# Expert mixture of a transformer block: all eight experts for every token, or only each token's two experts, with rows routed on the chip

## The reference

```python
x = x + layernorm(attention(layernorm(x)))     # 16 heads, causal, ALiBi, projection w_proj
x = x + layernorm(ffn(layernorm(x)))

def ffn(x):                                    # 2048 tokens
    scores = sigmoid(xt @ gate_w.T)            # 8 experts
    _, sel = top_k(scores + expert_bias, 2)    # the two experts of each token
    # rows of xt times their score, sorted by expert, in bfloat16:
    # out_e = (silu(rows @ w1[e].T) * (rows @ w3[e].T)) @ w2[e].T, hidden width 352
    shared = silu(xt @ sw1.T) * (xt @ sw3.T) @ sw2.T      # float32
    return shared + (the two routed results of each token)
```

## Time and profile before

| what | value |
|---|---|
| time, median of 3 runs | 1047.0 us (1046.97 to 1048.84) |
| profiled execution: span from first to last instruction | 1044.3 us |
| PE busy | 960.0 us, 92% of the span |
| DVE, ACT, POOL busy | 550.3, 391.6, 195.1 us |
| stage three | 571.7 to 1044.3 us |

### The profile page before, as it was taken

How to read it: one execution, slowest core, us unless ns; L and a number is a source line. 1 busy time by engine, 2 the same in 40 slices (tenths; PEclk the granted TensorE clock), 3 DMA queues, 4 the chain that set the end, 5 groups by cost and what they waited for, 6 DMA issues and landing times.

```text
span 1044.3 us, 15975 instructions
## 1 busy us (share of the span) xinstructions
PE 960.0 (92%) x5053; PEld 527.7 (51%) x5080; DVE 550.3 (53%) x1238; ACT 391.6 (38%) x690; POOL 195.1 (19%) x151
## 2 busy tenths in 40 slices
PE   4999996899999999999998799999999899999994
PEld 4787764344444444444433464446444554446442
DVE  6444466556565655556325343845456644745554
ACT  4121211365656555565627320432123421442221
POOL 4200034142232223232010030103110130103000
PEclk9999998899999999999999899999999999999997
DMA  9999483533635333345220500114001130102001
GB/s 275 277 276 293 160 240 119 109 85 81 138 75 118 81 82 82 83 97 155 66 96 12 183 21 0 41 41 141 20 7 74 40 121 0 56 24 81 1 1 40
DMA packets 71105, 101.55 MB, mean 97 GB/s; under 512 B 25616, under 2 KB 38544, under 8 KB 70032
## 3 DMA queue, kind: packets, MB, share of 16 engines
q1 hardware_dynamic: 59264, 92.02, 30.4%
q0 software_dynamic: 11792, 8.95, 5.5%
HBM read 75.81 MB, written 33.69 MB: 105 GB/s over the span
## 4 chain that ended last, share of the span: by engine, by line
PE 74%; DVE 4%; issue 4%; DMA 1%; ACT 1%; SPq 1%; DVEq 0%; ACTq 0%
PE ps L1254 24%; PE ps L1353 13%; PE ps L1267 9%; PE ps L1437 8%; PE ps L1333 8%; PE ps L1456 4%; PE ps L1468 2%; PE ps L1336 2%; PE ps L1368 2%; PE ps L1484 1%; DMA k_st<-qk_split 1%; DVE scb_c L1148 1%; PE ps L1462 1%; DVE ps L965 0%; DMA iota_c<-in_iota 0%
## 5 line engine op out<-in xcount | busy, mean ns | idle before, releaser
L965 DVE CUSTOM_DVE_ANT_0 ps<-ps,alibi 128x1024 f32<-128x1024 f32 (+7 forms) x256 | 190.9, 779 | 148.1 <-PE ps L1267 144.3
L814 ACT ACTIVATE probs<-ps,key_bias 128x512 f32<-128x512 f32 (+3 forms) x384 | 201.3, 577 | 161.7 <-PE ps L1336 109.7
L1254 PE MATMUL ps<-xs,w13r 128*128 128x512 bf16 (+1 forms) x744 | 171.3, 379 | 3.0 <-PE ps L1456 0.9
L898 ACT ACTIVATE silu<-ps 128x512 f32<-128x512 f32 (+1 forms) x108 | 64.0, 595 | 274.5 <-PE ps L1254 274.4
L1353 PE MATMUL ps<-probs,ones 128*32 128x512 f32 (+3 forms) x768 | 164.1, 502 | 0.0
L1353 PE MATMUL ps<-probs,v_st 128*32 128x512 f32 (+3 forms) x768 | 164.1, 502 | 0.0
L678 POOL TENSOR_SCALAR alibi<-rel_b,slp 128x1024 f32<-128x1024 f32 x32 | 91.1, 2848 | 322.6 <-DVE rowmax L965 224.2
L1267 PE MATMUL ps<-k_st,q_st 96*128 96x512 f32 (+3 forms) x384 | 112.8, 384 | 22.5 <-DVE rowmax L965 13.2
L1333 PE MATMUL ps<-q_st,k_st 98*128 98x512 f32 (+3 forms) x384 | 126.2, 394 | 7.5 <-ACT probs L814 3.6
L1212 DVE TENSOR_TENSOR gr<-silu,ps 128x512 bf16<-128x512 f32 (+1 forms) x96 | 65.5, 685 | 117.9 <-PE ps L1254 112.9
L1254 PEld LDWEIGHTS ps<-xs,w13r 128*128 128x128 bf16 (+1 forms) x768 | 80.8, 106 | 89.6 <-issue 6.1
(11 more groups left out here) (125 smaller groups left out, 1130.6 us busy)
## 6 DMA issues: line engine op xcount, KB each, us to landing
qk_split<-qk_out SPq DMA_DIRECT2D x32, 512.0 KB, 7.7
q_st<-qk_split SPq DMA_DIRECT2D x48, 256.0 KB, 4.6
k_st<-qk_split SPq DMA_DIRECT2D x48, 256.0 KB, 6.5
w13r<-in_w POOLq DMA_DIRECT2D x16, 352.0 KB, 34.2
x_a<-in_x SPq DMA_DIRECT2D x4, 1024.0 KB, 8.0
v_rows<-v_out SPq DMA_DIRECT2D x16, 256.0 KB, 3.7
v_st<-v_rows SPq DMA_DIRECT2D x16, 256.0 KB, 6.9
attended<-raw SPq DMA_DIRECT2D x16, 256.0 KB, 5.8
```

Source lines behind the costliest of these rows:

```text
L814: act.activation(probs[:, v % 3, e, 0:width], ps[:, score_bank(v, e), 0:width], ACT.Exp, bias=key_bias[par][:, 2 * pair + e, j - 4 * qc + ...
L898: act.activation(silu[0:r, t % 2, :], ps[0:r, bank, :], ACT.Silu).then_inc(c_silu, 1)
L965: dve.tensor_tensor_reduce(scores, scores, alibi[h % 2][:, S - width:S], 1.0, -3e38, ALU.add, ALU.max, rowmax[:, h, i:i + 1]).then_inc(b_m ...
L1254: last = pe.matmul(dst, lhsT, rhs, start=start and n == 0, stop=stop and n == len(terms) - 1)
```

## The change

Tokens are no longer sent through all eight experts. For every chunk DVE computes, beside the two experts and their scores, the rank of each token among the tokens of its expert (PE makes the running counts with a triangular matrix of ones, unit `rank`), and from it a row in a DRAM region of that expert (`pos`). DVE writes the token's activations, scaled by the score, in bfloat16 (`xs`: eight tiles of 128 rows a chunk), and POOL scatters each tile with an indirect DMA. After all four chunks DVE works out a table (`table`): for each of 23 tiles of 256 rows, its expert and its first row. The number of tiles is fixed, for any distribution of the tokens. Then the unit `experts` runs: SP reads a row number from the table, loads the tile transposed, PE reads the expert's number and multiplies by that expert's weights, addressed by a register; ACT and DVE each copy half of the result to bfloat16 and SP stores it. Ranks are turned into rows of the result (`result_rows`) during this time. Last, POOL gathers each token's two result rows with eight indirect DMAs a chunk, DVE adds them to the shared expert's result, normalises, and POOL adds the residual.

The shared result of chunks 0 to 2 is kept in DRAM meanwhile (`keep`); the shared expert of chunk 3 is computed after the experts. The loop over chunks is written out as one list, `PLAN`. Nine more DMAs on POOL near the start write zeros into the regions. Attention and the stage before it are otherwise untouched.

The core of the diff (added lines; what they replace are the units in the section on the kernel before):

```diff
-FIRST = [("tr", 0), ("tr", 1), ("gate",), ("logits",)]
...
+TS = 256
+TILES = (2 * B * S + E * (TS - 1)) // TS
+REGION = TS + B * S
...
+PLAN = [("tr", 0, 0), ("tr", 0, 1), ("proj", 1, 0), ("hilo", 0), ("gate", 0), ("proj", 1, 1),
+        ("logits", 0), ("norm", 1, 0), ("root", 1, 0), ("route", 0), ("hid", 0, 0), ("norm", 1, 1),
+        ("x1", 1), ("rank", 0), ("pos", 0), ("xs", 0), ("hid", 0, 1), ("norm", 1, 3), ("norm", 1, 4),
+        ("root", 1, 1), ("heads", 2), ("hid", 0, 2), ("norm", 1, 5), ("sdown", 0), ("keep", 0),
+        ("tr", 1, 0), ("tr", 1, 1), ("hilo", 1), ("gate", 1), ("logits", 1), ("route", 1),
+        ("proj", 2, 0), ("proj", 2, 1), ("norm", 2, 0), ("root", 2, 0), ("heads", 3), ("hid", 1, 0),
+        ("norm", 2, 1), ("x1", 2), ("rank", 1), ("pos", 1), ("xs", 1), ("hid", 1, 1), ("norm", 2, 3),
+        ("norm", 2, 4), ("root", 2, 1), ("norm", 2, 5), ("proj", 3, 0), ("proj", 3, 1),
+        ("norm", 3, 0), ("root", 3, 0), ("hid", 1, 2), ("norm", 3, 1), ("x1", 3), ("sdown", 1),
+        ("norm", 3, 3), ("norm", 3, 4), ("root", 3, 1), ("keep", 1), ("tr", 2, 0), ("tr", 2, 1),
+        ("hilo", 2), ("gate", 2), ("logits", 2), ("route", 2), ("hid", 2, 0), ("norm", 3, 5),
+        ("rank", 2), ("pos", 2), ("xs", 2), ("tr", 3, 0), ("tr", 3, 1), ("gate", 3), ("logits", 3),
+        ("route", 3), ("hid", 2, 1), ("rank", 3), ("count",), ("pos", 3), ("table",), ("xs", 3),
+        ("hid", 2, 2), ("sdown", 2), ("keep", 2), ("experts",), ("hilo", 3), ("hid", 3, 0),
+        ("hid", 3, 1), ("hid", 3, 2), ("sdown", 3)]
...
+            def tile_in(s):
+                row = sp.value_load(tab_r[0:1, s:s + 1], min_val=0, max_val=ROWS - TS)
+                if s >= 3:
+                    sp.wait_ge(e_first, MT * (s - 2))
+                sp.dma_start_transpose(xsT[:, s % 3, :, :], xs_d[bass.ds(row, TS), :]
+                                       ).then_inc(xs_in[s % 3], 16)
+
+            for s in range(3):
+                tile_in(s)
+            for s in range(TILES):
+                sp.wait_ge(e_act, s + 1)
+                sp.wait_ge(e_dve, s + 1)
+                sp.dma_start(ro_d[TS * s:TS * (s + 1), :].rearrange("(h p) n -> p h n", p=P),
+                             ro[:, s % 2, :, :]).then_inc(ro_out[s % 2], 16)
+                if s + 3 < TILES:
+                    tile_in(s + 3)
...
+                elif u[0] == "xs":
+                    for n in range(2 * TT):
+                        wait_alone(pool, c_xs, 2 * TT * u[1] + n + 1)
+                        k, t = n // TT, n % TT
+                        pool.indirect_dma_start(
+                            out=xs_d[:, :],
+                            out_offset=bass.IndirectOffsetOnAxis(place_c[:, u[1], k, t:t + 1], 0),
+                            in_=xs_rows[u[1]][:, k, t, :], in_offset=None).then_inc(xs_out, 16)
...
+            pool.wait_ge(rows_done, CHUNKS)
+            for c in range(CHUNKS):
+                if c:
+                    wait_alone(pool, f_added, c)
+                for n in range(2 * TT):
+                    k, t = n // TT, n % TT
+                    pool.indirect_dma_start(
+                        out=gathered_c[:, k, t, :], out_offset=None, in_=ro_d[:, :],
+                        in_offset=bass.IndirectOffsetOnAxis(result_c[:, c, k, t:t + 1], 0)
+                        ).then_inc(f_rows, 16)
+
+                wait_alone(pool, f_y, c + 1)
+                wait_alone(pool, f_x1, 16 * (c + 1))
...
+            def final(c):
...
+                dve.wait_ge(f_rows, 16 * 2 * TT * (c + 1))
+                for t in range(TT):
+                    if c == 3:
+                        dve.wait_ge(c_down, TT * c + t + 1)
+                    src = y[:, t, :] if c < 3 else ps[:, t, :]
+                    last = dve.tensor_tensor(y[:, t, :], src, gathered_c[:, 0, t, :], ALU.add)
+                cc.link(dve, last)
+                for t in range(TT):
+                    last = dve.tensor_tensor(y[:, t, :], y[:, t, :], gathered_c[:, 1, t, :], ALU.add)
+                last.then_inc(f_added, 1)
...
+            def experts():
...
+                e = expert_number(0)
+                for s in range(TILES):
+                    pe.wait_ge(xs_in[s % 3], 16 * (s // 3 + 1))
+                    for m in range(MT):
+                        n, r = MT * s + m, MROWS[m]
+                        if n >= 4:
+                            pe.wait_ge(e_gr, n - 3)
+                        for k in range(2):
+                            for d in range(DC):
+                                last = pe.matmul(
+                                    ps[0:r, 4 + n % 4, k * TS:(k + 1) * TS],
+                                    w13r[:, bass.ds(e, 1), k, d, m * P:m * P + r]
+                                    .rearrange("p o n -> p (o n)"),
+                                    xsT[:, s % 3, d, :], start=d == 0, stop=d == DC - 1)
+                        last.then_inc(e_first, 1)
+                        if m == 1 and s + 1 < TILES:
+                            following = expert_number(s + 1)
+                    if s:
+                        expert_down(s - 1, previous)
+                    previous, e = e, following
```

More of the change, by code:

```diff
@@ L71, in constants @@
         "future": np.where(k > q, np.float32(MASKED), np.float32(0)),
-        "iota": np.broadcast_to(np.arange(E, dtype=np.float32), (P, E)).copy(),
+        "lists": np.broadcast_to(listed(), (P, LISTED)).copy(),
+        "upper": np.where(k < q, np.float32(1), np.float32(0)),
     }
@@ L237, with slot, bank, used @@
+SEATED = [u for u in PLAN if u[0] in ("tr", "proj", "gate", "logits", "hid", "rank", "count")]
+ROOTS = [(0, 0), (0, 1)] + [u[1:] for u in PLAN if u[0] == "root"] + [(c, 2) for c in range(CHUNKS)]
+def slot(u):
+    return SEATED.index(u) % 2
+def bank(u):
+    return 4 + 2 * slot(u)
+def used(u):
+    return SEATED.index(u) + 1
+def freed(u):
+    return SEATED.index(u) // 2 + 1
+def root_of(c, n):
+    return ROOTS.index((c, n)) + 1
 A_CHAIN = 3
 NORM_AT = 3
-C_CHAIN_FIRST = 6
-C_CHAIN_PROLOGUE = 7
@@ L920, in _ @@
+            for c in range(CHUNKS):
+                root(root_of(c, 2))
         @block.vector
@@ L1249, in _ @@
+            for c in range(CHUNKS):
+                final(c)
         @block.tensor
```

977 lines of the change are left out of this document (586 added, 391 removed).

## The result

The changed kernel took 1075.8 us (median of 4 runs, 1071.9 to 1077.9) against 1047.0 us before: 1.027 times as long, with a 95% interval of 1.024 to 1.029. The forecast was 1074 us, in a range of 1018 to 1128. Its profiled execution has a span of 1075.5 us.

A forecast was written before the change was run, and what follows sets the result against it. PE's work was taken to bound stage three, with waits growing as it shrinks: first tile at 797 us, tiles 137, end 137 make 1071, with a 2.7 us offset 1074 us; range 1018 to 1128.

The forecast's parts named there:

- The first part: From PE's start at 597.4 us to the first tile at 797: 144 us of PE's work plus 56 of waits.
- the 6 for the clock: First part, within the 56 us: PE's slower clock costs 3 us at the start and 3 in chunk 2.
- 144 us of work: PE's work in the first part: gates, three projections, shared hidden pieces and second layers, transposes, ranks and logits.
- P: Period from tile to tile, max(W, (W + 2.1 + L) / 2): 5.95 us, 137 us for 23 tiles.
- W: PE's own time for one tile, with register instructions and load: 5.2 us, ends 3.9 and 6.2.
- 2.1: Tile loop, after PE's second layer: 0.65 us copy, 0.4 store issue, about 1 for register load and waits.
- L: Landing time of a tile's transposing load: 4.6 us, taken from a plain load of 256 KB.
- The end: From the end of the tiles to the span's end: 24.3 us, four chunks 108, last store 4.7; 137 us.
- T: Time one indirect DMA holds POOL: 1.1 us, between 0.77 (a plain DMA) and twice that.
- X: The end of the tiles, forecast at 934 us, from which the third part is counted.
- the rivals: Cheap gathers with feeds in time, 1031 us (0.27); slow transposed loads, 1136 us (0.12); dear indirect DMAs, 1118 us (0.10).
- 20 x T: How far the first part moves with T: 7 us down or 9 up.

The follow-up runs named there:

- a known expert and the loads first: Changed kernel with tile s's expert taken as s // 3 at build time and SP's load of tile s + 3 ahead of tile s's store: 1044.3 us.
- two buffers: Changed kernel with a second buffer for the rows gathered at the end, and gathers of chunks 0 and 1 issued together: 1035.9 us.
- the experiment: Changed kernel with the nine zero-writing DMAs moved on POOL from the start to behind attention's first tables: 1074.9 us.
- the gather ahead: Kernel with four edits, and POOL gathers chunk c + 2's rows ahead of chunk c's residual addition: 1003.3 us.
- four edits: Changed kernel with two gather buffers, first gathers ahead of chunk 3's low halves, chunk 1's heads early and tile loads first: 998.5 us.
- the expert known beforehand: Changed kernel with the expert of tile s taken as s // 3 at build time, so PE loads no register: 1061.9 us.

## Why the prediction was right

**What bounds the kernel** was PE's work, and the routed part was to shrink to 90 us if nothing else mattered. Shown: with a known expert and the loads first the tiles run at 3.92 us, 23 x 3.92 = 90 us. What the changed kernel takes beyond its work is waits, as the forecast said, and the lower clock behind them.

**The first part, 209.4 us for 199.6.** Here a size was off. The waits held: 209.4 - 159.7 = 49.7 us where the forecast's 56, without the 6 for the clock in it, are 50. Chunk 0's two low halves waited 11.7 us (forecast 12), the projection in chunk 1's part 5.5 (5), and the wait before the first tile was 6.0 (7). The term that was mis-sized is the clock, 3 us at the start and 3 in chunk 2: PE was busy for 159.7 us, of which by the rows some 143 are the forecast's "144 us of work" and 17 the clock. The granted clock was 0.85 in this part, against 1.00 in a full chunk of before, and at its lower level, 0.50, from 599 to 603 us and from 797 to 802, behind the waits of 19.6 and 7.4 us. The groups of the changed kernel, 599 to 808.4 us (columns as in the earlier trace rows), and two rows of PE's timeline show what it costs:

```profile
L1767 PE MATMUL ps<-wp_c,att_c 128*128 128x512 f32 x96 | 46.6, 645 | 25.1 <-POOL att_c L835 25.1
...
L1782 PE MATMUL ps<-xT,gate_c 128*8 128x512 f32 x32 | 19.2, 755 | 9.7 <-ACT xT L1045 9.7
```

```profile
800.50 0.63 PE L1522 MATMUL ps<-s_hi,g_lo 96*128 96x512 f32 x1
800.92 0.63 PE L1522 MATMUL ps<-s_hi,g_hi 96*128 96x512 f32 x1
```

The projections took 46.6 us where they took 42.2 before, the gates 19.2 instead of 4 x 3.6 = 14.4, and the last second layer runs at 0.42 us a product against 0.23, all right behind waits. The rows together, each against the same work at full clock: first projection 2.7 us, the two halves of chunk 0's second layer behind their waits 4.0, the two slow gates 4.8, chunk 3's transposes 1.7, the projections behind the wait of 5.5 us 1.3, the last part of the last second layer 2.5: 17.0. Waits cost twice here, once themselves and once by the clock behind them.

**The tiles, 5.45 us for 5.95.** The mechanism was right: P = (W + 2.1 + L) / 2, with each tile's load behind the store. Of its terms, 2.1 held (872.2 to 874.26) and W in this loop was 5.3, first layer 3.9 and second 1.4. L was mis-sized: mostly 3.4 us (up to 5.1 in single tiles), not 4.6. Half of that difference is 0.6 us a tile, the whole error (0.5, 12 us over the 23). By the forecast's working, the Trainium skill, DMA: Bandwidth & Descriptors ("Latency and other measured facts" and "Anatomy of one DMA"), gave an estimate of 3.0 us, and it was the nearer, though the page states the 2.0 us in it for DMAs that GpSimd issues and this load is SP's. W as PE's own pace, 5.2 us in the forecast, was wrong too, but didn't matter while the loop was the bound: PE alone needs 4.4. The other section of the Trainium skill that it weighed, TensorE: Matmul & The Clock Gate, "Wait — 56ns, not 53.3ns?", had come to about 4 if matmuls alone pay the sequencer's time; the page states its 62 ns for hardware decoding switched off, which the forecast left out. The runs gave 3.92 without registers and 4.38 with them, nearer to it than to my 5.2, and 24 pairs of weights and product in 2.78 us, 0.109 each, leave no room for two such times in a pair.

**The end, 141.8 us for 137.** T was 1.25 us and not 1.1: 0.95 for the instruction and 0.30 before the next. With 32 gathers in the tail that alone would be 4.8 us, 32 x 0.15, but it is the same number by chance. The four chunks took 27.8, 28.8, 27.7 and 27.6 us, 3.9 more than forecast, since the rest of a chunk was a little shorter; the first gather came at X + 23.6 (24.3), and the last store took 6.3 us to the end of the span, not 4.7, for a reason that no row shows. POOL's addition took 4.92 (5.0), DVE from start to norm 10.8 (10.7), as forecast; two buffers gave 40 us back and so showed that it was order and not transfer.

**Zeros and attention.** The forecast had nothing, at most 3 us, and the end of attention was 3.3 us late; by the experiment and the starts in the other kernels it isn't the zeros, so their term of nothing stands. What made the 3.3 us was not found.

The errors were +1.6, +9.8, -11.7 and +4.8 us. They cancel, and that is luck: the sum is 4.5 us under the span, and the forecast within 2 us of the median, because a part too long stood against two too short, while single parts were off by up to 12. One step in the rivals doesn't fit the forecast's own rule either: 20 x T would move the first part by 5 us for T = 0.85 and 18 for T = 2, where 3 and 15 are added; it decides nothing, since neither came true.

## What to carry to other kernels

Work taken from the bounding engine counts only as far as the remaining work still overlaps: here 139 us of PE's work went and the span grew by 31, so 170 us of idle time came. Read each queue as a list and ask of each instruction what it stands behind; one line of SP's loop, a load asked for before a store, was worth 24.6 us, though the waits named for it, without the one ahead of the first tile, were 5.2. Before moving an instruction back, look for who writes where it reads: the scatters cost more when they were late than when they were in the way.

## What the runs showed of the hardware

- DVE's and POOL's additions of float32 rows in SBUF hinder each other nearly wholly: four of them take 6.64 and 8.25 us at the same time, 2.50 and 4.92 apart. The Trainium skill, SBUF — State Buffer, "SBUF: two separate sides", says that GpSimd and a VectorE operation with two inputs in SBUF share a pair of ports by an exclusive lock; the trace agrees. In the kernel with the gather ahead even a DVE instruction on four numbers a partition (946.74 us), 0.17 us elsewhere, took 3.89, up to the end of POOL's additions. One gather of POOL beside DVE's additions (923.64 us in the kernel with four edits) took 3.33 us instead of 0.95, but those beside the first additions with two buffers (965 to 970 us) took 0.95 to 1.18; what decides this stays open.
- An indirect DMA of 128 rows holds POOL for 0.95 us, and the next begins 0.30 us later.
- A transposing load of 256 KB was issued in 1.25 us of SP's queue, and PE started on it 3.3 to 3.6 us after the issue began in 13 of 20 tiles, up to 5.1 in the others.
- A register instruction on PE's queue takes 46 ns by its row, and a load of a register from memory about 0.30 us; together they cost 0.46 us a tile while PE's queue is ahead, and right after a wait the third piece of a tile starts 0.5 us late besides (not so with the expert known beforehand).
